# A recurrence interleaved with windowed attention on one core: a new issue order, a nine-operation inverse root, a root and a mask issued in pieces

## What is computed

```python
x = x + 0.5 * ffn(layernorm(x))          # pass 1: 6 layers, windowed attention + gated MLP
x = x + lstm(layernorm(x))               # 1024 steps, one after another
x = x + 0.5 * ffn(layernorm(x))          # pass 2: the same 6 layers and weights
x = x + 0.5 * moe(layernorm(x)); x = x + attention(layernorm(x)); x = x + 0.5 * moe(layernorm(x))

def step(carry, inp):                    # lstm: one step, H = 128, 2 batch rows
    h, c, n = carry
    i_t = sigmoid(xi_t + h @ Wih); f_t = sigmoid(xf_t + h @ Wfh)
    g_t = tanh(xg_t + h @ Wgh);    o_t = sigmoid(xo_t + h @ Woh)
    c_t = f_t * c + i_t * g_t
    n_t = f_t * n + i_t * exp(g_t @ Weg + beg)
    h_t = o_t * (c_t / n_t)

# one ffn layer: 16 heads of 64, windows of 32 that see themselves and the window before
q, k, v = split(shift_tokens(x) @ Wqkv); q = rope(l2norm(q) * qs); k = rope(l2norm(k) * ks)
x = softmax(mask(q @ k.T * 8)) @ v @ Wo + x
x = (a * gelu(gate)) @ W2 + b2 + x       # a, gate = split(layernorm(shift_tokens(x)) @ W1 + b1)
```

## Time and profile before

| | us |
|---|---|
| median of 3 runs (5558.52 to 5566.41) | 5558.66 |
| the profiled execution, its time | 5569.78 |
| the profiled execution, its span | 5567.7 |
| main loop before the recurrence (to 1011.8) | about 900 |
| recurrence, first h to last h | 3187.8 |
| main loop after it, to about 5000 | about 800 |
| the other blocks | about 570 |

### The profile page before, as it was taken

One profiled execution on the slowest core, in us unless ns is written; L12 is line 12 of the kernel. 1 busy time (PEld: TensorE's weight loads), 2 busy tenths in 40 slices (PEclk: granted clock), 3 DMA queues, 4 the chain that ended last, 5 costly groups with the idle time before them and its releaser, 6 DMA issues. The chain is left out here.

```text
span 5567.7 us, 142026 instructions
## 1 busy us (share of the span) xinstructions
PE 5125.2 (92%) x51507; PEld 3368.9 (61%) x51508; DVE 4521.1 (81%) x15132; ACT 2971.0 (53%) x7179; POOL 2370.0 (43%) x2224
## 2 busy tenths in 40 slices
PE   4999999999999999998999999999998999997778
PEld 2555555666666676666666676666665555554353
DVE  4888888888888888888888888888888888885837
ACT  2666666555555555554555555555545666664030
POOL 2666666443333334333333333333335666662000
PEclk6999999999999999999999999999999999998888
DMA  3111101100000000000000000000000000000000
GB/s 118 34 37 33 36 12 42 32 18 18 14 18 17 15 17 15 26 6 20 5 26 13 19 18 18 14 18 19 13 18 22 26 30 30 30 7 11 2 0 18
DMA packets 106580, 123.22 MB, mean 22 GB/s; under 512 B 55014, under 2 KB 87480, under 8 KB 98872
## 3 DMA queue, kind: packets, MB, share of 16 engines
q1 hardware_dynamic: 105788, 114.34, 6.5%
q10 hardware_dynamic: 124, 0.03, 0.0%
HBM read 91.28 MB, written 23.07 MB: 21 GB/s over the span
## 5 line engine op out<-in xcount | busy, mean ns | idle before, releaser
L1610 POOL TENSOR_TENSOR t<-t 128x1024 f32<-128x1024 f32 x192 | 453.7, 2363 | 987.5 <-DVE t L959 987.5
L533 PE MATMUL banks<-h,lent 128*128 128x64 f32 (+11 forms) x6144 | 861.2, 277 | 0.4 <-DVE banks L908 0.4
L607 PE MATMUL banks<-Wvo,xq 128*32 128x512 f32 x6144 | 820.4, 605 | 6.1 <-ACT Vw L1313 2.0
L1603 POOL TENSOR_TENSOR t<-t 128x1024 f32<-128x1024 f32 x192 | 454.1, 2365 | 811.5 <-DVE t L959 811.5
L533 PEld LDWEIGHTS banks<-h,lent 128*128 128x128 f32 x6144 | 777.7, 194 | 2.0 <-DVE banks L908 0.7
L530 PEld LDWEIGHTS banks<-h,lent 128*128 128x128 f32 x2048 | 326.8, 191 | 508.5 <-DVE h L940 455.0
L1313 ACT COPY Vw<-banks 128x512 f32<-128x512 f32 x768 | 450.9, 587 | 315.4 <-PE banks L607 303.9
L1236 ACT ACTIVATE ge<-banks 128x2 f32<-128x2 f32 x1024 | 175.9, 172 | 827.0 <-PE banks L530 815.5
L954 DVE TENSOR_TENSOR t<-banks,rl 128x1024 f32<-128x1024 f32 x384 | 468.6, 1220 | 109.5 <-ACT sq L1268 66.6
L1618 POOL TENSOR_TENSOR t<-t,rnorm 128x1024 f32<-128x1024 f32 x192 | 365.9, 1906 | 375.8 <-DVE rnorm L111 369.0
L530 PE MATMUL banks<-h,lent 128*128 128x64 f32 (+7 forms) x2048 | 408.4, 281 | 120.5 <-DVE h L940 117.4
(11 more groups left out here) (314 smaller groups left out, 10588.5 us busy)
## 6 DMA issues: line engine op xcount, KB each, us to landing
Wqk<-in_L_ffn_Wqkv SPq DMA_DIRECT2D x24, 1024.0 KB, 5.1
Wvo<-wvo_kept SPq DMA_DIRECT2D x18, 1024.0 KB, 4.9
rl<-tables SPq DMA_DIRECT2D x24, 512.0 KB, 3.6
W<-in_L_ffn_W SPq DMA_DIRECT2D x24, 341.0 KB
tables<-tables SPq DMA_DIRECT2D x6, 1024.0 KB
wvo_kept<-Wvo SPq DMA_DIRECT2D x6, 1024.0 KB, 5.2
v_kept<-Vw SPq DMA_DIRECT2D x24, 256.0 KB, 2.5
Vw<-v_kept SPq DMA_DIRECT2D x24, 256.0 KB, 2.6
```

Of the source, the lines that this page charges most:

```text
L533: last = pe.matmul(ending(sb, to, 6, n, gate), c.Wg[:, gate + 1, 1, :], h.to_broadcast([P, n, B]), start=False, stop=True, skip_group_chec ...
L607: last = pe.matmul(vp[WIN * hq:WIN * hq + WIN, :], c.xq[n % 4][:, WIN * w:WIN * w + WIN], c.Wvo[stage % 2][:, hq, :], start=True, stop=True)
L1603: pool.tensor_tensor(t1, t1, t2[:, :], ALU.add).then_inc(s.q_sum, 1)
L1610: pool.tensor_tensor(t1, t1, t2[:, :], ALU.add).then_inc(s.k_sum, 1)
```

## The change

In `rsqrt_steps` the first two refinement rounds of three operations become one of four with a polynomial in y*y*v, so that the root has nine operations; it can be issued as part 0 (five operations) and part 1 (four). In the lstm step the product with Weg and the third sigmoid gate's are issued with 2 columns; the g product and the first two gates keep up to 64. The mask is laid by four products of 32 weight columns. `y_normalise` and `b_normalise` become four calls each: statistics, root part 0, root part 1, normalise. The calls between the steps are re-dealt on TensorE, VectorE, ScalarE and GpSimd, and the recurrence starts one step call later (`FIRST_SLOT` 29).

```diff
-NEWTON = 11
+NEWTON, FIRST_OF_NEWTON = 9, 5
+CUBIC = 0.6127962418008075, -2.0433132272690373, 1.8766156262487985
...
-    for _ in range(3):
+    scale, linear, constant = CUBIC
+    if part != 1:
+        step(first())
+        step(dve.tensor_scalar(y.bitcast(I32), v.bitcast(I32), -0.5, RSQRT_SEED, ALU.mult, ALU.add))
+        step(dve.tensor_tensor(t, y, y, ALU.mult))
+        step(dve.scalar_tensor_tensor(out=t, in0=t, scalar=scale, in1=v, op0=ALU.mult, op1=ALU.mult))
+        step(dve.scalar_tensor_tensor(out=t, in0=t, scalar=linear, in1=t, op0=ALU.add, op1=ALU.mult))
+        assert k == FIRST_OF_NEWTON
+    if part != 0:
+        step(dve.scalar_tensor_tensor(out=y, in0=t, scalar=constant, in1=y, op0=ALU.add, op1=ALU.mult))
         step(dve.tensor_tensor(t, y, y, ALU.mult))
         step(dve.scalar_tensor_tensor(out=t, in0=t, scalar=-0.5, in1=v, op0=ALU.mult, op1=ALU.mult))
         step(dve.scalar_tensor_tensor(out=y, in0=t, scalar=1.5, in1=y, op0=ALU.add, op1=ALU.mult))
...
-FIRST_ITERATION, FIRST_SLOT = 24, 28
+FIRST_ITERATION, FIRST_SLOT = 24, 29
...
         for gate in range(3):
-            last = pe.matmul(ending(sb, to, 6, n, gate), c.Wg[:, gate + 1, 1, :], h.to_broadcast([P, n, B]), start=False, stop=True, skip_group_check=True)
+            wide = n if gate < 2 else 1
+            last = pe.matmul(ending(sb, to, 6, wide, gate), c.Wg[:, gate + 1, 1, :], h.to_broadcast([P, wide, B]), start=False, stop=True, skip_group_check=True)
...
-        pe.matmul(ending(ge, at, 4, m, 1), c.Weg[:, :], c.ge[:, 0, :].unsqueeze(1).to_broadcast([P, m, B]), start=False, stop=True, skip_group_check=True).then_inc(s.e_done, 1)
+        pe.matmul(ge[:, at + B:at + 2 * B], c.Weg[:, :], c.ge[:, 0, :], start=False, stop=True, skip_group_check=True).then_inc(s.e_done, 1)
...
-        pe.matmul(sc[:, half * 512:(half + 1) * 512], c.identb[:, :], c.mask[:, t, :].unsqueeze(1).to_broadcast([P, 8, KEYS]),
-                  start=True, stop=False, skip_group_check=True)
+        for w in range(NW):
+            pe.matmul(sc[WIN * w:WIN * w + WIN, half * 512:(half + 1) * 512], c.identb[:, WIN * w:WIN * w + WIN],
+                      c.mask[:, t, :].unsqueeze(1).to_broadcast([P, 8, KEYS]), start=True, stop=False, skip_group_check=True)
...
+    def y_statistics(f):
...
+        dve.wait_ge(s.y_taken, past + 1)
+        aggregates(c.ysq, c.yrow[:, :], s.y_stat, s.y_aggr, c.ystat, 2 * past)
+
+    def y_root(f, part):
...
+        if part == 0:
+            dve.wait_ge(s.y_aggr, 2 * past + 2)
+        rsqrt_of(dve, s.y_newton, NEWTON * past, c.ysq[:, :], c.floor[:, FFN_STATS:FFN_STATS + 2 * GROUP],
+                 c.gv[:, :], c.gr[:, :], c.gt[:, :], part)
...
-        norm_probs(i - 5, 1)
         add_h(f)
-        move_k(i - 3)
         norm_q(i - 3)
+        norm_k(i - 3)
         add_q(i - 2)
```

More of the change, by code:

```diff
@@ L68, in band_mask, with rsqrt_steps @@
     return np.where(seen, 0.0, NEG).astype(np.float32)
[L71 to L86, removed]
-    for _ in range(3):
[L88 to L98, removed]
+def rsqrt_steps(dve, done, at, y, v, t, first, part=None):
+    k = 0 if part != 1 else FIRST_OF_NEWTON
     def step(instruction):
@@ L111, in rsqrt_of @@
         step(dve.scalar_tensor_tensor(out=y, in0=t, scalar=1.5, in1=y, op0=ALU.add, op1=ALU.mult))
-    assert k == NEWTON
+        assert k == NEWTON
+def rsqrt_of(dve, done, at, total, floor, v, y, t, part):
+    rsqrt_steps(dve, done, at, y, v, t,
+                lambda: dve.scalar_tensor_tensor(out=v, in0=total, scalar=1e-24, in1=floor, op0=ALU.max, op1=ALU.add), part)
 def is_zero(t):
@@ L822, in tensor_program @@
         step()
+        values(i - 4, 0)
         turn_q(i - 3, 0)
-        values(i - 4, 0)
         step()
         attend(i - 5, 1)
+        values(i - 4, 1)
+        turn_output(i - 5)
+        step()
         turn_q(i - 3, 1)
+        project_k(i - 2, 0)
         step()
-        turn_output(i - 5)
-        values(i - 4, 1)
+        make_weights(f - 1, 0)
         project(f - 1)
-        step()
-        project_k(i - 2, 0)
         project_k(i - 2, 1)
@@ L857, in tensor_program @@
         attend(i - 4, 1)
+        values(i - 3, 1)
         step()
-        values(i - 3, 1)
         y_back(f - 1)
-        step()
-        b_rows(f - 1)
         project_k(i - 1, 0)
         project_k(i - 1, 1)
+        turn_output(i - 4)
+        b_rows(f - 1)
         step()
-        turn_output(i - 4)
         values(i - 3, 2)
@@ L871, in tensor_program @@
         values(i - 3, 3)
-        turn_q(i - 2, 1)
+        turn_k(i - 2, 0)
         step()
         make_weights(f - 1, 1)
-        turn_k(i - 2, 0)
+        turn_q(i - 2, 1)
         b_back(f - 1)
@@ L997, in squares_k, with norms @@
         dve.tensor_reduce(c.ssq[:, HEADS:2 * HEADS], heads(sq[:, INNER:]), AX.X, ALU.add).then_inc(s.k_ssq, 1)
-    def norms(n):
+    def norms(n, part):
         g = n // 2 - LATER
@@ L1003, in norms @@
             return
-        if tile_ok(n):
+        if part == 0 and tile_ok(n):
             dve.wait_ge(s.q_ssq, n + 1)
             dve.wait_ge(s.k_ssq, n + 1)
-        if n % 2 == 0 and pair_ok(g):
+        if part == 0 and n % 2 == 0 and pair_ok(g):
             dve.wait_ge(s.f_aggr, 2 * (g + 1))
@@ L1177, in vector_program @@
         step()
+        squares_q(i - 2)
+        step()
         rotate_k(i - 2, 0)
@@ L1180, in vector_program @@
         rotate_k(i - 2, 1)
-        step()
-        squares_k(i - 2)
         statistics(f - 3)
         step()
-        norms(i - 2)
+        y_statistics(f - 1)
+        squares_k(i - 2)
+        step()
+        norms(i - 2, 0)
+        norms(i - 2, 1)
+        y_root(f - 1, 0)
         step()
@@ L1202, in vector_program @@
         step()
+        b_root(f - 1, 0)
+        b_root(f - 1, 1)
         b_normalise(f - 1)
+        rotate_k(i - 1, 1)
+        step()
         row_sums(i - 3)
         invert(i - 3)
-        step()
-        rotate_k(i - 1, 1)
         squares_k(i - 1)
         step()
-        norms(i - 1)
+        norms(i - 1, 0)
+        norms(i - 1, 1)
         step()
@@ L1473, in scalar_program @@
         step()
+        take_values(i - 4, 0)
+        step_g()
+        take_q(i - 3, 0)
+        step()
+        take_output(i - 5)
         exponent(i - 4)
@@ L1505, in scalar_program @@
         step()
-        square_q(i - 1)
-        take_probs(i - 4, 1)
+        take_probs(i - 4, 0)
         step_g()
         step()
+        square_q(i - 1)
+        step_g()
+        step()
+        take_probs(i - 4, 1)
         step_g()
@@ L1706, in pool_program @@
         add_k(i - 1)
+        shift(i + 1)
         norm_probs(i - 3, 0)
-        shift(i + 1)
-        norm_k(i - 1)
+        move_k(i - 1)
+        norm_probs(i - 3, 1)
 def sync_program(sp, c, s):
```

108 lines of the change are left out of this document (59 added, 49 removed).

## The result

The changed kernel takes 5461.77 us (median of 4 runs, 5453.02 to 5467.44) against 5559.9 for the kernel before in the same comparison: a ratio of 0.9818, interval 0.9806 to 0.983. The forecast was 5470, range 5395 to 5585. The time was forecast well, but not by its terms: of the four behind it one was right (the inputs), one came near in size with the wrong cause (outside the recurrence), and two were wrong in opposite directions (ordinary iterations, y and b).

What follows compares the result with a forecast made beforehand. TensorE bounds the kernel outside the recurrence; inside, the step's ring plus 5.5 us of surplus an iteration. Terms -10, -28, -22 and -30 make -90 from 5569.78: 5480, scaled to the runs' median and taken as 5470, range 5395 to 5585.

Steps and rivals of the forecast that it cites:

- the inputs: The lstm's inputs' product moved from fill 4 to the head of fill 5: -3.7 us in each of six iterations, -22.
- outside the recurrence: Iterations ahead of and behind the recurrence: TensorE's wait for GpSimd's `norm_q` covered, mask cheaper; together -30 us.
- ordinary iterations: 49 iterations of the recurrence: new order and narrow products together -0.2 us each, -10 in all.
- y and b: Their normalisations cut into pieces over several fills: -3.5 us in each of eight iterations, -28.
- The ring: Each step's chain from h back to h: narrow last gate saves 0.03 us in 16 of 21 intervals, 0.5 an iteration.
- the rival's: Ring follows the last product alone, 0.08 us, and POOL meets no part of y or b: 5400, chance 0.13.
- the order alone loses 0.35: Fills of an ordinary iteration in the new order: surplus 5.85 us against 5.5, the root's saving included.
- Part 0 can meet a POOL operation (0.74): y's root part 0 behind fill 9 on VectorE: 1.15 us, possibly held 0.74 by GpSimd, 1.9 together.
- I see no new wait: Outside the recurrence, with the wait for `norm_q` covered, `norm_k` and `turn_k` are next late but add no wait.
- The mask's term: The scores' mask in four narrow products side by side: -0.25 us an iteration in 41, -10; ends -20 and +87.
- The clock rival: In the step, narrow products leave TensorE idle, clock falls to 0.50, 0.86 us a step: 5617, chance 0.08.
- The POOL rival: GpSimd's bunched order holds VectorE's fills in three or four more places an iteration, 0.74 us each: 5597, chance 0.12.

Runs made afterwards that it cites:

- e4: The changed kernel with all three gates' products at 2 columns, only the g product widened: 5570.15 us, ratio 1.0012.
- e2: The changed kernel with the third gate's product and the product with Weg both back at up to 64 columns: 5486.32 us, ratio 0.9863.
- e3: The changed kernel with the product with Weg alone back at up to 64 columns: 5466.19 us, ratio 0.9829.
- e5: The kernel before with the root of nine operations alone, in one part: 5521.74 us, ratio 0.9923.
- e7: The changed kernel with the mask laid by one product of 128 columns again: 5474.95 us, ratio 0.9842.
- e8: The changed kernel with y's parts together in fill 12 and b's in fill 16: 5448.36 us, ratio 0.9793.
- e9: The changed kernel with y's root parts moved from fills 9 and 12 to fill 10 and the start of fill 11: 5417.1 us, ratio 0.9743.
- e12: The kernel before with the inputs' product moved to the head of fill 5 and ScalarE's copies one call later: 5545.38 us, ratio 0.9970.
- e6: The changed kernel with GpSimd's calls in the order of the kernel before: 5454.19 us, ratio 0.9803.
- e1: The kernel before with the third gate's product and the product with Weg alone at 2 columns: 5567.14 us, ratio 1.0009.
- e10: The kernel of e9 with GpSimd's calls in the order of the kernel before: 5417.22 us, ratio 0.9735.
- e11: The kernel before with the third gate's product alone at 2 columns: 5540.91 us, ratio 0.9964.

## Why the prediction held, term by term

That the time came within 8 us is in part luck. The sum of -90 was made against the profiled execution, and the two profiled ones differ by 116.7. Two terms missed by 46 and 21 us in opposite directions, and most of what was left went into the gap between profiles and medians.

1. **The ring: mis-sized, and undone elsewhere if done alone.** 0.03 was forecast, 0.052 measured. Two things were wrong. The 0.04 of the earlier trace rows is one pair of steps at two decimals: the quickest steps of the kernel before take 1.328 from h to `es` with 34 columns and 1.353 with 64, a difference of 0.025. And I spread it over the columns of three products. Only the last product's count: in the changed kernel the quickest steps take 1.301 whatever the columns of the others, and e4 agrees. 0.025 for 30 columns is 0.052 for 62; that reading, with 0.08, was the rival's. "16 of 21 intervals" came out (e2), but by another way: the third gate shortens eleven, and the product with Weg, for which I counted nothing, the five that TensorE ends (e3). The term was forecast as 24 us and e2 measures 24.5. That is chance: 0.76 instead of 0.5 in an ordinary iteration would be 37 in 49, and the profiles do not show where the difference went. The Trainium skill, "TensorEngine Tiling (Array Packing)", section "Instruction Overhead", has one column take as long as 60. No run agrees for the product that the engine waits for: 62 columns less gave 0.052 us, and from 34 to 2 columns the quickest steps still went from 1.328 to 1.301. For the two ahead of it, e4 agrees as far as the ring goes.
2. **Ordinary iterations: -0.2 forecast, -1.14 measured.** The lengths of the intervals were close, and none was forecast too short:

| interval | before | forecast | measured |
|---|---|---|---|
| 3 | 2.73 | 3.27 | 3.13 |
| 7 | 2.74 | 3.17 | 3.17 |
| 9 | 4.23 | 3.81 | 3.51 |
| 13 | 2.73 | 3.17 | 3.10 |
| 14 | 2.92 | 2.98 | 2.93 |
| 17 | 3.51 | 3.84 | 3.76 |
| 18 | 4.82 | 4.34 | 4.10 |

Interval 9 met GpSimd in none of the 34 ordinary iterations, so the 0.4 added for that was not there; 18 was 0.24 shorter. (The list in the prediction adds up to 5.90, not 5.85.) With wide products (e2) an ordinary iteration is 5.1 us above 21 undisturbed steps, where 5.85 was forecast, and the narrow ones give 0.76, where 0.5 was. That makes the 0.9 us an iteration, some 46 us in 49, that I left on the table. The step that failed is "the order alone loses 0.35", in which the root's saving was counted: in e2 the order, the root and the mask together win 0.38. The root alone wins 0.51 (e5) and the mask about 0.1 (e7), so, if they add, the moved calls lose some 0.2 in these iterations.

3. **y and b: the step failed.** -28 was forecast, and about -7 is what seven of these eight iterations gained beyond an ordinary one's gain. "Part 0 can meet a POOL operation (0.74)" was the wrong price and the wrong word: the operation is the one that the norms themselves start, so it is met always, and it holds VectorE for 1.6 us, not 0.74. "If the low clock goes with the idle time" did not come true either: interval 9 became the half idle one. e8 shows that these pieces won nothing over the pile, and e9 that the idea was right and the place wrong.
4. **The inputs: right.** -3.7 in each was forecast; the mean surplus of 33, 39, 51, 57 and 63 went from 5.1 to 1.5. e12 shows the mechanism alone, with 16 of the 22 us; there both halves of a projection stayed in fill 5.
5. **Outside the recurrence: near in size, wrong cause.** -30 was forecast for 41 iterations. The 21 ahead and the 22 behind give -18.2; -28.9 is reached only with the pipeline's filling and emptying (-7.0 and -3.7), which no term named. I credited the order of the calls with the wait of the earlier trace rows, GpSimd's above all. The wait goes without GpSimd's order (e6). Behind the recurrence the root gives 8.4 (e5) and the mask 5.6 (e7), which together are 14.0 of the measured 13.9, so that nothing is left for the order. The step of this term that failed is "I see no new wait": TensorE's waits in eight iterations of the changed kernel, where GpSimd no longer appears, come to 10.5 us, more than the 6.3 of the earlier trace rows:

```profile
PE banks L697 <- DVE xB L1055: 4.9, 8, 0.6
PE banks L578 <- ACT KT L1324: 3.7, 8, 0.5
PE banks L626 <- DVE xA L1173: 1.9, 8, 0.2
```

The mask's term, -10, measured 11 outside the recurrence, for which it was made, and 13 in all. Ahead of the recurrence the sum stays open: root (4.1 in e5) and mask (5.6) make more than the 4.3 measured, so something in the new order costs about 5 there; it isn't GpSimd's order, which is 3 better than the old one.

6. **The rivals.** The clock rival had the right mechanism at the wrong place: the profile of the changed kernel does not show it in ordinary iterations, but its two narrow products meet it in the old order (e1), two more narrow ones in the new order (e4), and e6, e7, e9 and e10, each one edit or two away, in one to three iterations. The new order and the two narrow products belong together: apart, e2 gives 76 and e1 nothing; together 98. It is the product with Weg that needs the new order, as the third gate alone gives 21 in the old one (e11). The POOL rival was there at one place (interval 18, 0.31) and in y, not at three or four. The parts measured alone add up to 41 (root) + 21 (third gate) + 16 (inputs) + 13 (mask) = 91 of 98, if they add; the mask's was measured in the new order, the others in the old.

## What to carry to other kernels

Ahead of putting work "behind" a long operation, look at what that operation releases on other engines: here the freed engine started at once and blocked the very work that was put there, while one fill later there was nothing to collide with. A shorter ring is worth what the clock leaves of it: ask what the removed columns did for TensorE's activity in the emptiest fills. When a forecast comes out right, cut the result by stage all the same; here two terms were off by 21 and 46 us in opposite directions. And a mean over iterations can hide a few in which the clock fell: set the median beside it.

## What the runs showed of the hardware

- Of three products in a row into one wait, only the last one's columns delay the waiting engine: 62 columns less there brought `es` 0.052 us earlier, 124 less ahead of it 0.000 (medians over all steps of the changed kernel and e4).
- A VectorE operation on 4 columns took 1.77 us instead of 0.17 while GpSimd multiplied 128x1024 (1.90 us), and ended with it.
- 62 columns of a product that was not late decided the granted clock: in the old order without them it fell in seven of the 34 ordinary iterations (to 0.53 and 0.67 in the intervals 13 and 14 of iteration 34), and it stayed at 1.00 in all 34 with them (e1, e11). Which iterations it takes is not settled: neighbours with the same work kept 1.00.
